# Value products of three steps together, narrow output transposes and a later ternary quantisation in a two-layer attention kernel

## The reference

```
layer 0:
  q = LN(x);          x = x + MHA(q, q)              # 16 heads of 8 channels
  qc = LN(x); kv = LN(ctx)
  x = x + MHA(qc, kv)                                 # 56 queries against 1500 keys
  x = x + top-2-of-8 experts(LN(x))                   # 128 -> 512, gelu, 512 -> 128
layer 1:
  q = LN(x) @ T(Wq).T + bq;  k = ctx @ T(Wk).T + bk;  v = ctx @ T(Wv).T + bv
  x = x + softmax(q k / sqrt(8)) v @ T(Wo).T + bo
T(W) = clip(round(W / (g + 1e-5)), -1, 1) * g,  g = mean |W|     # ternary weights
```

## Time and profile before

| | |
|---|---|
| median of 3 runs | 633.04 us (632.65 to 633.94) |
| the profiled execution | 633.05 us |
| its span, first to last instruction | 631.3 us |
| mean granted TensorE clock | 0.929 |
| TensorE busy | 542.5 us, 86% |
| VectorE busy | 389.0 us, 62% |
| ScalarE busy | 326.4 us, 52% |
| GpSimd busy | 199.1 us, 32% |

### The profile page before, as it was taken

How to read it: one execution, slowest core, us unless ns; L and a number is a source line. 1 busy time by engine, 2 the same in 40 slices (tenths; PEclk the granted TensorE clock), 3 DMA queues, 4 the chain that set the end, 5 groups by cost and what they waited for, 6 DMA issues and landing times.

```text
span 631.3 us, 16157 instructions
## 1 busy us (share of the span) xinstructions
PE 542.5 (86%) x6582; PEld 386.4 (61%) x6582; DVE 389.0 (62%) x974; ACT 326.4 (52%) x495; POOL 199.1 (32%) x190
## 2 busy tenths in 40 slices
PE   0699838799999999979968989378999999999996
PEld 0587515566666767747736767145666766767774
DVE  5668479677777776776234211578777677676720
ACT  1265214456767677635733333225666666666572
POOL 2553214647594854400025100224041240330000
PEclk9899769889999999979987999778999999999997
DMA  5010621634554435412200731026537437353300
GB/s 155 34 51 1 164 76 44 166 75 128 136 130 117 130 77 145 93 50 57 100 1 3 177 108 60 25 69 153 132 91 185 119 86 178 86 144 84 72 3 16
DMA packets 36987, 58.66 MB, mean 93 GB/s; under 512 B 16308, under 2 KB 20524, under 8 KB 36916
## 3 DMA queue, kind: packets, MB, share of 16 engines
q1 hardware_dynamic: 36916, 57.66, 36.1%
HBM read 17.81 MB, written 0.23 MB: 29 GB/s over the span
## 4 chain that ended last, share of the span: by engine, by line
PE 54%; issue 23%; DVE 11%; DMA 5%; POOL 3%; ACT 2%; SPq 2%; DVEq 0%; POOLq 0%; ACTq 0%
PE SM L1209 11%; PE PO L1224 11%; PE ST L1181 7%; PE MI L1123 6%; PE MI L1133 6%; DVE mxp L824 5%; PE MI L1157 2%; PE MI L1112 2%; DMA cx<-in_ctx 2%; PE SM L1296 2%; DMA qst<-mrow 1%; ACT ksplit L598 1%; PE SM L1157 1%; DVE cstat L796 1%; SPq L361 1%
## 5 line engine op out<-in xcount | busy, mean ns | idle before, releaser
L824 DVE TENSOR_REDUCE mxp<-SM 112x1 f32<-112x500 f32 x364 | 237.5, 674 | 92.0 <-PE SM L1209 91.2
L626 ACT ACTIVATE PT<-ST 128x896 f32<-128x896 f32 x192 | 171.3, 912 | 57.7 <-PE ST L1181 57.5
L1209 PE MATMUL SM<-kst,qst 96*112 96x500 bf16 x364 | 141.5, 403 | 16.8 <-DVE mxp L824 12.5
L1181 PEld LDWEIGHTS ST<-qst,kst 98*128 98x128 bf16 x1536 | 94.8, 100 | 37.2 <-issue 13.6
L1181 PE MATMUL ST<-qst,kst 98*128 98x112 bf16 x1536 | 108.9, 215 | 1.8 <-DMA qst<-mrow 1.8
L500 POOL TENSOR_TENSOR kr<-kf,ksplit 128x500 f32<-128x500 f32 x48 | 54.3, 1134 | 149.3 <-ACT ksplit L598 149.3
L1224 PE MATMUL PO<-PT,vaug 125*32 125x112 f32 x3072 | 98.0, 266 | 2.1 <-ACT PT L626 1.5
L1224 PEld LDWEIGHTS PO<-PT,vaug 125*32 125x32 f32 x3072 | 71.7, 111 | 24.9 <-issue 16.2
L1209 PEld LDWEIGHTS SM<-kst,qst 96*112 96x112 bf16 x364 | 46.9, 131 | 48.8 <-DVE mxp L824 31.8
L610 ACT ACTIVATE vaug<-MI 125x512 f32<-125x512 f32 x48 | 28.7, 598 | 77.4 <-PE MI L1133 77.4
L505 POOL TENSOR_TENSOR ksplit<-kr,ksplit 128x500 bf16<-128x500 f32 x48 | 54.6, 1138 | 41.7 <-DVE ksplit L819 41.7
(11 more groups left out here) (131 smaller groups left out, 544.0 us busy)
## 6 DMA issues: line engine op xcount, KB each, us to landing
kst<-ksplit SPq DMA_DIRECT2D x192, 187.5 KB, 3.8
cx<-in_ctx SPq DMA_DIRECT2D x8, 750.0 KB
xT<-in_ctxT SPq DMA_DIRECT2D x8, 750.0 KB, 5.1
moe<-in_w1T SPq DMA_DIRECT2D x8, 256.0 KB, 2.9
moe<-in_w2T SPq DMA_DIRECT2D x8, 256.0 KB, 3.0
qall<-qsplit SPq DMA_DIRECT2D x12, 112.0 KB, 2.3
qst<-qall SPq DMA_DIRECT2D x56, 21.0 KB, 1.9
watt<-in_watt SPq DMA_DIRECT2D x1, 768.0 KB, 5.3
```

Of the source, the lines that this page charges most:

```text
L626: nc.scalar.activation(PT[:, k % PTB], ST[:, k % 2, :, 0:4 * PC], ACT.Exp, scale=SCALE).then_inc(exp_done, 1)
L824: nc.vector.tensor_reduce(mxp[:, j // 3, j % 3:j % 3 + 1], tile_bank(j, banks), AX.X, ALU.max).then_inc(sm_red, 1)
L1181: last = mm(ST[:, k % 2, cc, PC * p:PC * (p + 1)], kst[n.par][:, 4 * half + p, at:at + 128], qst[n.par][:, 4 * half + p], start=True, stop ...
L1209: mm(tile_bank(j, banks), qst[n.par][0:SROWS, j // 3], kst[n.par][0:SROWS, j // 3, at:at + THIRD], start=True, stop=True).then_inc(sm_full, 1)
```

## The change

It has four parts. (1) `values` runs for three steps together, at steps 0, 3, 6 and 9; the exponentials have six slots, four in `PT` and two in the part of `moe` in which the experts' hidden layer lies at other times. (2) `transpose_po` writes only the 36 meaningful columns of each product, packed, and `normalise` reads them so. (3) The output transposes move from step 3 to step 7, behind the value projection; the normalisation stands at step 8 behind its first tile, `output_forth` at step 9. (4) The ternary weights move from step 6 of unit 5 to step 0 of unit 7.

```diff
-PTB = 4
+PTB = 6
+GROUP = 3
-K_STEP, BACK_STEP, V_STEP, FORTH_STEP, CTX_STEP = 0, 3, 4, 7, STEPS - 3
+K_STEP, V_STEP, BACK_STEP, FORTH_STEP, CTX_STEP = 0, 4, 7, 9, STEPS - 3
...
-        PT = sb("PT", [128, PTB, 2, 4 * PC])
+        PT = sb("PT", [128, 4, 2, 4 * PC])
...
+        spare = moe[:, 4 * DFF:].rearrange("k (b c x) -> k b c x", b=2, c=2)
+
+        def pt(k):
+
+            slot = k % PTB
+            return PT[:, slot] if slot < 4 else spare[:, slot - 4]
...
-                nc.scalar.activation(PT[:, k % PTB], ST[:, k % 2, :, 0:4 * PC], ACT.Exp, scale=SCALE
+                nc.scalar.activation(pt(k), ST[:, k % 2, :, 0:4 * PC], ACT.Exp, scale=SCALE
...
-                heads = bank[0:L].rearrange("q (h x) -> q h x", x=32)
+                heads = back[0:L, 0:H * VW].rearrange("q (h x) -> q h x", x=VW)
...
-                    if k == BACK_STEP and (n + -1).exists():
+                    if k == BACK_STEP + 1 and (n + -1).exists():
                         normalise_unit(n + -1)
...
-                    if n.s == 0 and n.c == B - 3 and k == HSTEP:
+                    if n.s == 0 and n.c == B - 1 and k == 0:
                         ternary_weights()
...
+                rows_of = ident[:].rearrange("k (p x) -> k p x", x=32)
                 for half in range(2):
                     for hh in range(2):
-                        at = 256 * half + (128 - VW) * hh
-                        last = mm(bank[0:L, at:at + 128], po[:, PC * half + L * hh:PC * half + L * (hh + 1)],
-                                  ident[:], start=True, stop=True, skip_group_check=True)
+                        at = 4 * VW * (2 * half + hh)
+                        last = mm(back[0:L, at:at + 4 * VW], po[:, PC * half + L * hh:PC * half + L * (hh + 1)],
+                                  rows_of[:, :, VW * hh:VW * (hh + 1)], start=True, stop=True,
+                                  skip_group_check=True)
...
-                    if k % 2 == 0 and (k or prv.exists()):
+                    if k % GROUP == 0 and (k or prv.exists()):
                         of = n if k else prv
-                        values(of, (k - 2) % STEPS)
-                        values(of, (k - 1) % STEPS)
+                        for back in range(GROUP, 0, -1):
+                            values(of, (k - back) % STEPS)
...
-                values(last, STEPS - 2)
-                values(last, STEPS - 1)
+                for back in range(GROUP, 0, -1):
+                    values(last, STEPS - back)
```

More of the change, by code:

```diff
@@ L851, in place_q, with normalise @@
                 last.then_inc(qst_ready, 1)
-            def normalise(bank, full, rden_sem, done, full_at, rden_at, par):
+            def normalise(back, full, rden_sem, done, full_at, rden_at, par):
                 dve.wait_ge(full, full_at)
-                heads = bank[0:L].rearrange("q (h x) -> q h x", x=32)
+                heads = back[0:L, 0:H * VW].rearrange("q (h x) -> q h x", x=VW)
                 nc.vector.reciprocal(rden[:], heads[:, :, DH]).then_inc(rden_sem, 1)
@@ L1149, in transpose_max, with transpose_po @@
                                     identb[0:PC, 0:PC]).then_inc(mx_full, 1)
-            def transpose_po(bank):
+            def transpose_po(back):
+                rows_of = ident[:].rearrange("k (p x) -> k p x", x=32)
                 for half in range(2):
                     for hh in range(2):
-                        at = 256 * half + (128 - VW) * hh
-                        last = mm(bank[0:L, at:at + 128], po[:, PC * half + L * hh:PC * half + L * (hh + 1)],
-                                  ident[:], start=True, stop=True, skip_group_check=True)
+                        at = 4 * VW * (2 * half + hh)
+                        last = mm(back[0:L, at:at + 4 * VW], po[:, PC * half + L * hh:PC * half + L * (hh + 1)],
+                                  rows_of[:, :, VW * hh:VW * (hh + 1)], start=True, stop=True,
+                                  skip_group_check=True)
                 return last
@@ L1224, in values @@
                         last = mm(PO[32 * p:32 * p + 32, PC * half:PC * (half + 1)], vaug[n.par][:, c, at:at + 32],
-                                  PT[0:KC, k % PTB, cc, PC * p:PC * (p + 1)], start=(k == 0 and cc == 0),
+                                  pt(k)[0:KC, cc, PC * p:PC * (p + 1)], start=(k == 0 and cc == 0),
                                   stop=(k % HSTEP == HSTEP - 1 and cc == 1), skip_group_check=True)
```

## The result

The changed kernel takes 642.68 us (median of 4 runs, 639.85 to 648.1) where the kernel before takes 632.85 on the same chip: ratio 1.0137, 95% interval 1.0091 to 1.0184. Against 633.04 us that is 641.7, on the slower side, near the upper end of the range given (624 to 642) and outside the 632 to 640 that the forecast's own case was given. Ratios leave out executions that took over 1.5% longer than the fastest of the same kernel; in experiment 2 these are four of ten, and with all ten its median is 633.4 us. The profiled execution has a span of 642.1 us, 10.8 more than before, so it can be read stretch by stretch.

What follows compares the result with a forecast made beforehand. TensorE's own queue was taken to set the time inside the units (busy 542.5 of 631.3 us). Savings, new waits and half clock summed to +2.6 us on 633.0: 635.5 us, range 624 to 642, own case 632 to 640.

Steps and rivals of the forecast that it cites:

- The new wait: Forth transpose at step 9: TensorE stands 0.97 us for two reductions and the normalisation, 1.7 in units 1 to 3.
- Rival 2: Forth transpose doesn't wait because reductions run ahead; 13 units gain 1.0 to 1.7 us, about 615; chance 0.10.
- Savings: Full second-pass unit: value threes -0.60, key projection's evacuation wait -0.51, narrow transposes -0.46, step 8 tile wait -0.36 us.
- Rival 4: Narrow transposes cost what they did, weight load 0.10 us: 8 us more, 643.5; chance 0.05.
- Ternary weights: Unit 5, first pass: moving them removes 4.12 us of waiting and some 2.2 lost at half clock, -6.6 us.
- queue term: First pass, units 1 to 3: head gains nothing, tail loses 2.1 to 2.2 us per unit, +6.6 us.
- clock term: Units 1 to 3: five of six waits of 1.6 to 1.7 us followed by half clock, about 1.2 each, +6 us.
- Rival 1: Clock stays up through the 1.6 us waits: 6 us less, 629.6; chance 0.25.
- rival 3: The 1.0 us waits halve the clock too: ten more, half of them at 1.2 us, 642; chance 0.10.
- The start: Self-attention: seven narrow transpositions on the chain gain 0.46 us each, -3.2 us.
- Unit 0: First pass, unit 0: reductions and context waits cost +0.5 us.
- Unit 6 of the first pass: Head bound by reductions, which hide the value group saved; no evacuation wait to remove: +0.65 us.

Runs made afterwards that it cites:

- experiment 2: Changed kernel with the normalisation ahead of step 8's tile reduction on VectorE; ratio 0.9927 to the kernel before.
- experiment 1: Changed kernel with the forth transpose one step later, at step 10; ratio 0.9857 to the kernel before, some 624 us.
- experiment 7: Changed kernel, forth transpose at step 10, context load behind key stacks: 0.9848; with 128-column self-attention transposes and the load moved only in units 1 to 3: 0.9757.
- experiment 6: Changed kernel with a SyncE wait in unit 0 of the first pass, holding unit 2's transfers until the row of maxima landed; ratio 1.0141.

## Why the prediction came out as it did

**The new wait.** Right, and the main thing. 0.97 us was predicted and 0.85 measured, at 9 transposes, and 1.7 and 1.41 at the 3 of units 1 to 3. Experiments 1 and 2 show that it is paid one for one in the second pass, and experiment 1 that it decides the sign. Rival 2 was right that without it the change would win, though its 615 was too low: on the changed kernel's other parts that gives 0.9857, 624 us.

**Savings.** Right in size in a full unit of the second pass: transposes 0.60 in TensorE's timeline (0.62 predicted), the key projection's wait gone, groups of three 0.39 a unit (0.6 predicted, part of it covered by tiles that wait for reductions). In the whole time the threes show no gain over pairs, since in the profile the first pass gives it back. Rival 4 fell.

**Ternary weights.** -6.6 predicted, 6.4 by ratio alone, 7.1 in the profile after.

**Units 1 to 3.** The mechanisms were right. I split the sum with experiment 7's kernel, whose TensorE is busy 76.08 us at full clock with much the same work: the changed kernel has 78.04, so by this estimate 2.0 us of it is clock and 9.2 - 2.0 = 7.2 are queues (6.6 predicted). The repeated execution gives 82.74, so 6.7 and 7.4. The queue term repeats; the clock term (6 predicted) is a different number in each execution. Five of the six waits halve the clock, the prediction said; one of six and four of six did. The length of the wait does not decide it: in the first profile the 2.27 us at 189.30 left the clock at 1.00 and the 1.41 at 199.38 did not. Rival 1 (nothing) and rival 3 (the waits of 1.0 too) lie on either side: of the 18 waits of 0.84 or 0.85 us in the two executions one was followed by half clock, that at 536.46, and cost 1.55 us. What decides between two equal waits stays open.

**The start.** The term -3.2 failed. Seven transposes by 0.46 was a sum over TensorE's work, but at one step the end is set by VectorE's normalised exponentials; the wait there took 0.93 us back at once, and the half clock behind it most or all of the rest (46.1 to 49.6 us for 46.6 to 47.0). In this profile 1.4 us of the row's miss of 4.0 lie ahead of the self-attention. A wait of 0.94 for them at this place stood in the kernel before, and the prediction did not use it.

**Unit 0.** The term +0.5 failed, by 4.5 us. I counted reductions and context transposes, not that TensorE reaches the end of step 5 sooner (2.2 us here), when 1.8 KB of maxima are still under way with the key stacks issued ahead of and behind them. The wait for them grew by 4.0 us. Why the row itself came 1.8 us later, and why executions of the same code in unit 0 fall to 29 or to 34 us, is not settled: the distance of the two issues goes with it in all profiles but one, and holding the later transfers back gained nothing.

**Unit 6 of the first pass.** +0.65 predicted, +2.5 in this profile, +0.9 in the repeated one (26.84 us, at full clock). The 0.9 is the forth transpose's wait; the other 1.6 goes with a stretch at half clock from 294.8 to 297.5 us:

```profile
293.62 0.42 PE L1219 MATMUL SM<-kst,qst 96*112 96x500 bf16 x1 [0.16 <-DVE mxp L832]
294.22 0.42 PE L1219 MATMUL SM<-kst,qst 96*112 96x500 bf16 x1 [0.19 <-DVE mxp L832]
...
294.00:298.00 4.00, 3.81 (x59) 3.03 (x58) 2.04 (x4) 1.11 (x2) 0.00 (x0) 0.57 0.45 99
```

No rival had this: the waits ahead of it are those for reductions, of 0.16 to 0.19 us each, and the forth transposes' waits stand 10 us before it and 10 behind.

The start (4.0), unit 0 (4.5) and unit 6 (1.9) less units 1 to 3 (3.4) make 7.0 of the 8.2 us between +2.6 and +10.8; the other rows together make the 1.2 left. So the time came out within the range with the sign for the predicted reason, but the size is in part luck: with the start and unit 0 as predicted the profile would show +2.3, close to the +2.6, and only because the clock term, too large by 4 in this profile, makes up for the other misses.

## What to carry to other kernels

A step table in which each edit wins can lose as a whole: after moving work, count what is left between a product and its first reader on the same engine, here 1.0 us of TensorE against two reductions and a normalisation. Give the reader one step more before giving up the edit: that was 17.7 us. And shortening one engine's work in a chain that another engine ends gave nothing here and cost its clock; read who released the next wait first. Last, try the parts alone: narrow transposes and late weights (0.9845) gave as much as the whole with its wait mended (0.9857).

## What was unexpected of the hardware

The same TensorE wait of 1.41 us was followed by a granted 0.57 in one execution (173.24) and by 1.00 in another of the same kernel (169.46); the mean granted clock of units 1 to 3 was 0.96, 0.91 and, with the hold of experiment 6, 0.89. The Trainium skill (TensorE: Matmul & The Clock Gate, "Why this matters for your kernels") warns of longer idle gaps only; here 1.41 us was followed by half clock four times in six, and the 1.87 us of the self-attention in all nine profiles, while 0.94 at the same place was in none of five. A stretch at half clock came with no wait above 0.19 us in the 10 us before it (unit 6). A transfer of 1.8 KB took 8.6 us with nothing issued behind it and 9.9 with key stacks issued 3.9 us behind, with a context load and six key-stack transfers issued in the 6.6 us ahead of it; in the kernel before it took 6.5.
